# A fused mixing-and-FFN kernel on one core: clip and floor of the mixing become checked sums, and its prefix weights and gate are made with exp alone

## The reference, cut to what matters

```python
tf = sigmoid(sum(time_emb, -1))
decay = exp(-exp(w)) * (0.5 + 0.5 * tf)
ek = exp(minimum(k, 30.0)); ekv = ek * v            # k = v = fside
# forward and reverse scans over the positions: a = a * decay + ekv_t; b = b * decay + ek_t
euk = exp(minimum(u + k, 30.0))
num = nf + nb - ekv + euk * v
den = df + db - ek + euk
base = sigmoid(r) * (num / maximum(den, 1e-08))     # r = x
mixed = base * (0.8 + 0.2 * tf)
h = einsum('bsd,fd->bsf', mixed, W1)
a = gelu(clip(round(h / 0.1), qmin, qmax) * 0.1)
out = x + einsum('bsf,df->bsd', a, W2)
```

## Time and profile before

| | |
|---|---|
| median of three executions | 1795.56 us |
| profiled execution | 1794.38 us, span 1791.5 us |
| mean granted TensorE clock | 0.985 |
| PE busy | 1696.8 us (95%) |
| DVE busy | 1177.8 us (66%) |
| ACT busy | 1071.3 us (60%) |
| DMA | mean 179 GB/s |

### The profile page before, as it was taken

The page is one execution under the profiler, slowest core; times in us unless marked ns, Lnnn a source line. Parts: engine busy times, 40 slices in busy tenths (PEclk is TensorE's granted clock), DMA queues, the critical chain, the costliest instruction groups (busy, mean ns, idle before and its releaser), DMA issues.

```text
span 1791.5 us, 27197 instructions
## 1 busy us (share of the span) xinstructions
PE 1696.8 (95%) x10882; PEld 1066.3 (60%) x10882; DVE 1177.8 (66%) x1737; ACT 1071.3 (60%) x1471; POOL 24.6 (1%) x44
## 2 busy tenths in 40 slices
PE   1379999999999999999999999999999999999998
PEld 0124444786458854687448864588546874488643
DVE  8977875688666675768765776677867676633211
ACT  5668752787348863598627873489635985245300
POOL 0000020000000000000000000000000000000000
PEclk9779999999999999999999999999999999999999
DMA  9857784755555644665547545556445655455442
GB/s 241 185 148 224 257 300 153 246 179 181 168 174 182 201 135 155 204 206 178 167 126 227 177 164 173 174 183 217 141 156 192 199 166 160 139 174 166 139 133 80
DMA packets 109234, 321.13 MB, mean 179 GB/s; under 512 B 12720, under 2 KB 12720, under 8 KB 108592
## 3 DMA queue, kind: packets, MB, share of 16 engines
q1 hardware_dynamic: 106416, 296.28, 51.2%
q0 software_dynamic: 2688, 23.07, 5.7%
HBM read 310.91 MB, written 48.23 MB: 200 GB/s over the span
## 4 chain that ended last, share of the span: by engine, by line
PE 74%; DMA 3%; DVE 3%; issue 1%; ACT 1%; SPq 0%; DVEq 0%; ACTq 0%
PE ps L519 38%; PE ps L575 36%; DMA x_in<-in_x_dram 2%; DMA chk_full<-in_w_dram 1%; DMA VP<-in_fside_dram 1%; DVE chk_full L1157 1%; ACT L677 0%; DVE y_out L1149 0%; DVE ND L1022 0%; DVE ND L1042 0%; DVE ND L1026 0%; DVE RCP L983 0%; ACT L684 0%; ACT RCP L678 0%; DVE ND L1047 0%
## 5 line engine op out<-in xcount | busy, mean ns | idle before, releaser
L575 PE MATMUL ps<-act,w_ring 128*128 128x512 f16 x4096 | 889.2, 379 | 4.3 <-DVE y_out L1149 4.3
L519 PE MATMUL ps<-mo,w_ring 128*128 128x256 f16 x6272 | 689.6, 273 | 2.8 <-ACT ps L720 2.5
L575 PEld LDWEIGHTS ps<-act,w_ring 128*128 128x128 f16 x4096 | 401.1, 98 | 484.2 <-issue 6.6
L519 PEld LDWEIGHTS ps<-mo,w_ring 128*128 128x128 f16 x6272 | 612.5, 98 | 81.0 <-issue 4.5
L1140 DVE SCALAR_TENSOR_TENSOR act<-a,act 128x1024 f16<-128x1024 f32 x128 | 156.2, 1221 | 159.8 <-ACT act L769 159.8
L1149 DVE SCALAR_TENSOR_TENSOR y_out<-ps,x_in 128x512 f32<-128x512 f32 x64 | 44.1, 690 | 197.2 <-PE ps L575 125.4
L777 ACT ACTIVATE q<-chk_full 128x1024 int8<-128x1024 f32 x64 | 67.0, 1047 | 144.5 <-DMA chk_full<-in_w_dram 144.5
L763 ACT ACTIVATE a<-q 128x1024 f32<-128x1024 int16 x128 | 135.4, 1057 | 15.4 <-DVE act L1140 11.1
L769 ACT ACTIVATE act<-a 128x1024 f16<-128x1024 f32 x128 | 134.2, 1049 | 0.9
L496 PE MATMUL ps<-mo,w_ring 128*128 128x512 f16 x128 | 42.0, 502 | 80.5 <-DVE mo L1075 80.5
L1157 DVE SCALAR_TENSOR_TENSOR chk_full<-q,chk_full 128x1024 f32<-128x1024 int8 x64 | 78.0, 1219 | 57.8 <-ACT q L777 57.8
(11 more groups left out here) (102 smaller groups left out, 1299.1 us busy)
## 6 DMA issues: line engine op xcount, KB each, us to landing
w_ring<-w1s SPq DMA_DIRECT2D x168, 512.0 KB, 3.7
w_ring<-w_half SPq DMA_DIRECT2D x144, 512.0 KB, 4.3
chk_full<-in_w_dram SPq DMA_DIRECT2D x64, 512.0 KB, 4.6
V<-in_fside_dram SPq DMA_DIRECT2D x64, 256.0 KB, 4.6
R<-in_x_dram SPq DMA_DIRECT2D x64, 256.0 KB, 5.0
w_half<-in_w_dram POOLq DMA_DIRECT2D x16, 1024.0 KB, 8.0
x_in<-in_x_dram SPq DMA_DIRECT2D x64, 256.0 KB, 5.6
out_dram<-y_out SPq DMA_DIRECT2D x64, 256.0 KB, 5.0
```

Of the source, the lines that this page charges most:

```text
L519: mm = pe.matmul(dst[:, f, :], wp_ring[:, k, r, f, q, :], mo[:, op, q, p, :], start=(fresh and f == 0 and q == 0 and p == 0), stop=(q == K ...
L575: mm = pe.matmul(y_ps[y][:, :], w2_ring[:, k, f, :], act[:, a, p, :], start=(a == 0 and p == 0), stop=(a == FT - 1 and p == 1))
```

## The change

The clip of EK and the floor of DEN go out of the tile (a sum over exp(-V), and one over exp(-R), are put in the verdict in their place). For a late tile ScalarE now makes exp of the prefix input itself and, apart from it, the decay weights exp(scale * RAMP), written into EKV's place; VectorE multiplies the two and sums up (L986), then multiplies with the input and sums up (L989). `prefix_argument` remains only in the general path. The gate is exp(-R), whose 1 + exp(-R) multiplies DEN, not NUM, so `reciprocal` now waits for the gate. EK and EKV lie in one tile EE (NUM and DEN were already in one tile ND), and one instruction of 1024 columns now adds the bonus to both. The square of V that only served the verdict becomes exp(-V). A table is loaded once ahead of a tile that stands between gelus, and not otherwise.

```diff
@@ exps
-                sc.preload_act_table_set(EXP_SET)
                 if late:
-                    act_e.wait_ge(s_arg, pg + 1)
-                    sc.activation(EKP[:, :], EKP[:, :], ACT.Exp, accum_out=pre_d[:, c:c + 1]).then_inc(s_ekp, 1)
+                    act_e.wait_ge(s_vp[pg % 2], 16 * (pg // 2 + 1))
+                    if pg > 0:
+                        act_e.wait_ge(s_decayed, pg)
+                    sc.activation(EKP[:, :], VP[:, pg % 2, :], ACT.Exp).then_inc(s_ekp, 1)
...
+                if late:
+                    act_e.wait_ge(s_ramp, 3)
+                    act_e.wait_ge(s_lndec, B + 1)
+                    sc.activation(EKV[:, k, :], RAMP[:, :], ACT.Exp, scale=lndec[:, b, c:c + 1]).then_inc(s_weight, 1)
...
-                sc.activation(RCP[:, :], V[:, k, :], ACT.Square,
+                sc.activation(RCP[:, :], V[:, k, :], ACT.Exp, scale=-1.0,
                               accum_out=vsum[:, g:g + 1]).then_inc(s_vsq, 1)
@@ reciprocal, tanh
-            def reciprocal(g):
-                act_e.wait_ge(s_den3, g + 1)
+            def reciprocal(g, done, count):
+                act_e.wait_ge(done, count)
...
-                sc.preload_act_table_set(EXP_SET)
...
-                sc.activation(R[:, g % 2, :], R[:, g % 2, :], ACT.Tanh, scale=0.5).then_inc(s_tanh, 1)
+                sc.activation(R[:, g % 2, :], R[:, g % 2, :], ACT.Exp, scale=-1.0,
+                              accum_out=rsum[:, g:g + 1]).then_inc(s_sig, 1)
...
+            def tile_group_between(g):
+
+                sc.preload_act_table_set(EXP_SET)
+                tile_group(g)
@@ weigh
                     dve.wait_ge(s_ekp, pg + 1)
-                    v.scalar_tensor_tensor(out=EKV[:, k, :], in0=EKP[:, :], scalar=1.0, in1=VP[:, pg % 2, :],
+                    dve.wait_ge(s_weight, pg + 1)
+                    v.scalar_tensor_tensor(out=EKV[:, k, :], in0=EKP[:, :], scalar=1.0, in1=EKV[:, k, :],
+                                           op0=ALU.mult, op1=ALU.mult, accum_out=pre_d[:, c:c + 1]).then_inc(s_decayed, 1)
+                    dve.wait_ge(s_decayed, pg + 1)
+                    v.scalar_tensor_tensor(out=EKV[:, k, :], in0=EKV[:, k, :], scalar=1.0, in1=VP[:, pg % 2, :],
                                            op0=ALU.mult, op1=ALU.mult, accum_out=pre_n[:, c:c + 1]).then_inc(s_dot, 1)
+                    dve.wait_ge(s_dot, pg + 1)
                 dve.wait_ge(s_ekx, g + 1)
-                v.tensor_scalar(EK[:, k, :], EK[:, k, :], EXP_CLIP, None, ALU.min).then_inc(s_ek, 1)
-                dve.wait_ge(s_ek, g + 1)
@@ sums
-                v.scalar_tensor_tensor(out=DEN[:, k, :], in0=EK[:, k, :], scalar=bonus[:, b, c:c + 1], in1=DEN[:, k, :],
-                                       op0=ALU.mult, op1=ALU.add).then_inc(s_den2, 1)
-                v.scalar_tensor_tensor(out=NUM[:, k, :], in0=EKV[:, k, :], scalar=bonus[:, b, c:c + 1], in1=NUM[:, k, :],
-                                       op0=ALU.mult, op1=ALU.add).then_inc(s_num2, 1)
-                dve.wait_ge(s_den2, g + 1)
-                v.tensor_scalar(DEN[:, k, :], DEN[:, k, :], floor[:, b, c:c + 1], None, ALU.max).then_inc(s_den3, 1)
-                dve.wait_ge(s_num2, g + 1)
-                dve.wait_ge(s_tanh, g + 1)
-                v.scalar_tensor_tensor(out=NUM[:, k, :], in0=R[:, k, :], scalar=1.0, in1=NUM[:, k, :],
+                v.scalar_tensor_tensor(out=ND[:, k, :, :], in0=EE[:, k, :, :], scalar=bonus[:, b, c:c + 1],
+                                       in1=ND[:, k, :, :], op0=ALU.mult, op1=ALU.add).then_inc(s_sums, 1)
+                dve.wait_ge(s_sums, g + 1)
+                dve.wait_ge(s_sig, g + 1)
+                v.scalar_tensor_tensor(out=DEN[:, k, :], in0=R[:, k, :], scalar=1.0, in1=DEN[:, k, :],
                                        op0=ALU.add, op1=ALU.mult).then_inc(s_gate, 1)
@@ part
-                    if g % CT < CT - 1:
-                        prefix_argument(g + 1)
```

More of the change, by code:

```diff
@@ L132, in adaln_ffn_kernel @@
         bonus = sb("bonus", [P, B, CT], F32)
-        floor = sb("floor", [P, B, CT], F32)
+        gap = sb("gap", [P, B, CT], F32)
         eu_sb = sb("eu_sb", [P, CT], F32)
@@ L141, in adaln_ffn_kernel @@
         vsum = sb("vsum", [P, TILES], F32)
-        verdict = sb("verdict", [P, 10], F32)
+        rsum = sb("rsum", [P, TILES], F32)
+        verdict = sb("verdict", [P, 13], F32)
         ones = sb("ones", [P, 1], F32)
@@ L601, in _ @@
                     output(n, d, 1)
-            pe.wait_ge(s_vote, 12)
-            pe.matmul(f_ps[0:1, 0:1], verdict[:, 9:10], ones[:, :], start=True, stop=True).then_inc(s_votes, 1)
+            pe.wait_ge(s_vote, 13)
+            pe.matmul(f_ps[0:1, 0:1], verdict[:, 0:1], ones[:, :], start=True, stop=True).then_inc(s_votes, 1)
             def general_block(m):
@@ L689, in tile_group @@
                 if g % CT:
-                    reciprocal(g - 1)
-                tanh(g)
+                    reciprocal(g - 1, s_gate, g)
+                gate_exp(g)
+            def tile_group_between(g):
+                sc.preload_act_table_set(EXP_SET)
+                tile_group(g)
             def mix_hi(g):
@@ L785, in _ @@
                     mix_hi(t - 1)
-                reciprocal(t)
+                reciprocal(t, s_gate, t + 1)
                 if t + 1 < CT:
-                    tanh(t + 1)
+                    gate_exp(t + 1)
             mix_hi(CT - 1)
@@ L857, in _ @@
                     operands_hi(n + 1, 2)
-                    reciprocal(g0 + 7)
+                    reciprocal(g0 + 7, s_gate, g0 + 8)
                 check_i8(at + 6)
@@ L879, in general_block @@
                     general_exps(g)
-                    reciprocal(g)
-                    tanh(g)
+                    sc.preload_act_table_set(EXP_SET)
+                    reciprocal(g, g_den3, g - TILES + 1)
+                    act_e.wait_ge(s_r[g % 2], 16 * (g // 2 + 1))
+                    sc.activation(R[:, g % 2, :], R[:, g % 2, :], ACT.Tanh, scale=0.5).then_inc(s_sig, 1)
                 for s in range(STEPS):
@@ L1160, in _ @@
             factors()
-            prefix_argument(0)
             for t in range(CT):
@@ L1193, in hidden_block @@
                     if nxt:
-                        if s == 0:
-                            prefix_argument(g0)
-                        elif s % 2 == 0:
-                            part(3, g0 + s // 2 - 1)
+                        if s % 2 == 0:
+                            if s > 0:
+                                part(3, g0 + s // 2 - 1)
                         else:
```

109 lines of the change are left out of this document (56 added, 53 removed).

## The result

The changed kernel takes **1776.47 us** (median of four, 1776.06 to 1777.35); the kernel before, run beside it, takes 1796.12 us (1794.16 to 1796.93). The ratio is 0.9893, with a 95% interval of 0.9876 to 0.991: about 1.1% faster, 19.65 us by the medians. The prediction was 1779.0 us with a range of 1775.5 to 1784; its main case alone had 1776.5 to 1781.5, so the median lies at the lower edge of that.

What follows compares the result with a forecast made beforehand. TensorE, 95% busy, bounds the kernel, so only its waits count, mainly for VectorE in block 0's mixing. 9.5 + 3.2 + 1.4 + 2.5 = 16.6 us off 1794.38 gives 1777.8, as median 1779.0 us, range 1775.5 to 1784.

Steps and rivals of the forecast that it cites:

- main case: Whole kernel: all terms hold as forecast, 1776.5 to 1781.5 us, chance 0.52.
- A tile of block 0: VectorE in block 0's mixing: carry to first scan falls from 6.35 to 5.14 us, 1.2 us less per tile.
- the rival with two passes: VectorE's 1024-column sum takes 2.55 us instead of 1.32, so only 3.5 us gained, 1792; chance 0.07.
- The start: Tile 0 of block 0: L986 starts at 8.8, the scan at 12.6, not 13.54, so 0.95 us earlier.
- the list of signs: Trace signs for or against the forecast, among them no VectorE idle time in front of L986 in block 0.
- The mixing: Block 0: TensorE's seventh `mix_lo` comes 9.5 us earlier, with 1 us kept each way for the clock.
- The wait for `residual_sum(0, 0)`: TensorE's 4.3 us wait at block 0's end shortens by 3.2 us, leaving 1.1.
- its low clock: TensorE behind the `residual_sum(0, 0)` wait: the clock stays up, saving 1.4 us, or 0 if it falls.
- The rival in which they stay: Block 0's end: weight-sum stores don't move, the wait shrinks 1.2 instead of 3.2, low clock stays; 1782.4, chance 0.24.
- The starts of the blocks: TensorE's four waits for ScalarE's `seed` at block ends vanish, 2.5 us.
- What costs nothing: Late tiles of later blocks: ScalarE's extra exp and VectorE's longer `weigh` are covered by `seed_u4`'s 77.2 us of waits.
- My rival on the slower side: `seed_u4` comes late in blocks 1, 3 and 5, twelve times; decides above 1.7 us each; 1796 to 1797, chance 0.05.

Runs made afterwards that it cites:

- e7: Changed kernel with the 1024-column sum split into two of 512: 1778.23 us, ratio 0.9906.
- e1: The changed kernel run again, unaltered, against the kernel before: 1776.59 us, ratio 0.9891.
- e6: Changed kernel with the four early converting transfers of W2 moved behind those of W1: 1775.7 us, ratio 0.9891.
- e11: Changed kernel with the prefix argument in one VectorE instruction, one product, and block 0's upper-half copy ahead of the next tile's exps: 1773.47 us, ratio 0.9873.
- e3: Changed kernel with the two extra table loads per tile back in blocks 1 to 7 only: 1788.26 us, ratio 0.996.
- e2: Changed kernel with three table loads per tile back in block 0's mixing only: 1777.3 us, ratio 0.9894.
- e4: Changed kernel with the EK clip and one pass over DEN back in block 0's eight tiles only: 1784.8 us, ratio 0.9933.
- e9: Changed kernel with the two extra table loads back only in the 24 late tiles of blocks 2, 4 and 6: 1782.75 us, ratio 0.9926.
- e10: Kernel before with only the gate as exp(-R) on DEN and the table loads this saves removed: 1787.74 us against 1796.29, ratio 0.9952.
- e8: Kernel before with only the new making of the prefix weights, all table loads kept: 1798.91 us against 1796.02, ratio 1.0018.
- e5: Changed kernel with the EK clip and one pass over DEN back in blocks 1 to 7 only: 1779.93 us, ratio 0.9914.

## Why the prediction was right, point by point

- **A tile of block 0, 1.2 us.** Right: 5.10 us against 5.14 forecast. The wide sum is one pass, 1.279 us; the rival with two passes (2.55 us) fell, and e7 bears that out: two halves cost 0.13 more, not less. The Trainium skill ("Vector Engine (DVE) Microarchitecture Reference", *7. Points that are easy to get wrong*), which was weighed for that rival, says that this shape halves throughput, but not against what. Against the plain product of two f32 sources it does not: 1.279 us here, 1.225 for L1097. Against an instruction with one f32 source both are slow: 0.74 and 0.69 us for 512 columns in the earlier trace rows, where the clip L972 takes 0.42. The sentence may mean that, and then the rows don't contradict it.
- **The start, 0.95.** Right: 1.01, but by two small errors that cancel. L986 starts at 9.01, not 8.8, since the decay weights' exp takes 0.72 us and not 0.63, and from there to the scan it is 3.52, not 3.77. VectorE idled 0.96 us in front of L986; the sum had most of that in it, although the list of signs said that there would be none.
- **The mixing, 9.5.** It was 8.6, and 9.2 in e1. The term that was too large is the one of six more intervals, 7.2: five of them gained 1.25 us each, and the one from tile 1's scan to tile 2's nothing (13.22 against 13.19). What I missed is one wait of 1.2 us there: ScalarE's exp of the next prefix input waits for its load, and a copy that VectorE needs is queued behind it. That interval couldn't be shorter because the input wasn't there. e6 and e11 take the wait away in two ways. The clock within the joint piece took another 0.86, inside the 1 us that I had kept.
- **The wait for `residual_sum(0, 0)`, 3.2, and its low clock, 1.4.** Right: 3.3 and 1.35. That the stores move with VectorE's sums was right as well: L707, now L722, moved from 230.82 to 218.02, 12.8 us, while the second product starts only 7.7 us earlier than before (197.45, 205.18). The rival in which they stay fell. They didn't set the time in either kernel: L710, now L725, waits for VectorE (1.26 us for L1086 before, 3.01 us for L1099 after). e3 brings both back with the loads alone, and e2 and e4, which act only in the mixing, don't, and neither does e9, which acts on the late tiles alone. So the cause, table loads in the tile groups that block 0 serves beside its products, is shown.
- **The starts of the blocks, 2.5.** Too small: 4.3. The mechanism was right (e10, with the gate and its loads alone, takes 3.3 of it away), but I priced it by the listed waits, and each of these is 0.16 us short of the late start that it stands for, and the small ones are missing. The starts of four blocks lost 3.6 us, not 2.5, and 0.7 was lost within blocks 1, 3 and 5, where I looked for nothing.
- **What costs nothing.** This step failed, and its failure is hidden in the total. I had covered the third exp with the 77.2 us that `seed_u4` waits for TensorE, and had spread them over 56 times. That is the number of instructions; the trace has 30 waits, so nearly half of them had no such cover. The instruction did stay covered here (it now waits 85.0, in 32 of 56). But VectorE idles 46.9 us in front of L986, in 19 places, and what comes late is not what I looked at: it is ScalarE's gelu, then VectorE's `act_lo`, the scans and `quantise22` behind them. e8 shows that the new prefix alone makes the kernel 2.9 us slower, e9 that two loads in the late tiles cost 6.2 us. The two changes meet in the same chain: the loads that go make the room that the exp fills. My rival on the slower side had the right blocks and named the wrong instruction behind; with the loads gone its point of decision is not reached.
- **The sum.** That 16.6 met 16.4 is partly luck. The mixing gave 0.9 less than forecast and the clock in the joint piece took another 0.9; the stretches gave 1.8 more.
- **The parts.** Put back or done alone, by medians: the gate and its loads 8.5 (e10), the two passes 8.2 + 3.3 (e4, e5), the wide sum 1.6 (e7), the prefix -2.9 (e8). That is 18.7 of the 19.3 to 19.7 us that the medians show. It proves little. The prefix costs its 2.9 only where the loads stand beside it, and by the spans of the profiled executions the same five differences make 11.0 of 16.4 us.
- **Open.** The 3 us between the 16.4 of the spans and the 19.65 of the medians, and what releases the three late starts within blocks 1, 3 and 5 of the kernel before.

## What to carry to other kernels

Price an edit by start-to-start time where nothing covers it, and elsewhere by the longest chain that ends at the busy engine: follow what is queued behind the edit on both engines, through gelu, scans and quantising, not only the next instruction that the busy engine needs. Measure what the busy engine lost between two fixed points of its program, not by its listed waits. Beside a TensorE that is 95% busy, two table loads a tile cost 11.7 us, and two VectorE passes 3.3. And try the parts alone: one of them (e8) made this kernel slower, and its replacement by an older form in one instruction (e11) gave another 3 us.
